# Reordering the head of a two-layer mixer: base chunk 0 ahead of later logits, sums of the weights moved off TensorE, the last group's mixing weights by GpSimd

## The chip, the cores and the metric

One core of one Trainium2 chip. The metric is the device time of one execution, in microseconds; lower is better. The engines are TensorE (PE, with its weight loads as PEld), VectorE (DVE), ScalarE (ACT), GpSimd (POOL) and SyncE (SP), which here only issues DMAs.

## The reference, cut to what matters

Input x has 64 samples of 32 rows (channels) and 512 columns. Two layers are added to it in turn, each a mixing of channels followed by a low-rank expert layer over the columns.

```
# layer 0: mixing weights from the condition of each sample
h = gelu(gelu(cond @ W0 + b0) @ W1 + b1);  att = softmax(h @ W2 + b2)          # [64, 8]
m = einsum('boi,bih->boh', sum_k att[b,k] * weight[k], x) + (att @ bias_k)[:, :, None]
# layer 0: linear layer and top-2 of 8 experts of rank 16
w = softmax over the two largest of  m @ gate_w.T
x = x + m @ base_w.T + base_b + 2 * sum_e w_e * (m @ lora_A[e].T) @ lora_B[e].T
# layer 1: grouped convolution of 9 taps along the columns, plus context, top-2 of 4 experts
m = conv1d(x, weight, groups=4, pad=4) + (cond @ c_weight.T)[:, :, None] + bias
x = x + 4 * sum_e gates_e * (m @ A[e].T) @ B[e].T
```

The mixing acts on the channels and the linear maps on the columns, so they can change places. The kernel multiplies x with `base_w`, `lora_A` and `gate_w` first and mixes the products. The bias of the mixing then contributes the product of a bias per channel and the sum of a weight's rows: the sums over the 512 inputs of `lora_A`/`gate_w` (`lg_sum`), of `base_w` (`sum_w`) and of layer 1's `A`/router (`pj_sum`).

## The kernel before, in words

The 2048 rows (64 samples of 32 channels) are cut into four groups (g or i, 0 to 3) of four tiles (t) of 128 rows; the 512 columns lie in four chunks (c) of 128. x comes in transposed, one DMA for each group and chunk. Nearly all products are taken in a split form: a tile is rounded to a "high" part (on ACT), the rest is the "low" part (VectorE or GpSimd subtract), and `hi_lo` (L959) issues three matmuls, lines L963 to L965. All order is written out by hand: each engine has one queue, waits on counting semaphores, and takes its instructions strictly in the order of the code.

The head, which the change touches, has these steps:

- The attention: `h1`, `h2` and `att` by TensorE with Gelu and Exp on ACT; `keep_busy` (L954) issues products without use between them. `attb` brings the attention weights to 128 partitions.
- `x_logits` (L972): x times lgw in full precision, group 0 only, tile by tile, needing all four chunks of x for each tile. `xl_out` (ACT) evicts them.
- `x_base` (L1020): x times base_w; for group 0 chunk by chunk, from high and low parts (`x_high`, `base_high` on ACT, `x_low`, `base_low` on VectorE). `p0_out` (L442, ACT) evicts it to `p0`.
- `mix_sum` and `mix_half` (L678, L685, VectorE): products of attention and weights and their reduction, which give the mixing matrices of a group; `mix_place` (L502, ACT) puts them into `mixT`. Group 0 is step 1, group 1 step 2, groups 2 and 3 two halves each.
- The sums: lgw by eight matmul instructions with a matrix of ones (L1206), base_w the same way (L1235), copied to a row and turned by L1243, the A/router rows by L1256.
- `mix_logits` (L982) mixes the logits; VectorE adds the bias in `logits` (L690) and runs the gate, `route0` (L698) with one Exp on ACT (`gate_exp`); `turn_lw` (L1034, TensorE line L1037) transposes the result `lw`, `lwT_high` and `lwT_low` split it.
- `x_first` (L998) is the part of the products with x of group 1 that holds the logits.
- `make_y` (L1076): for each chunk four mixes (`mix_base`, L1055) and the experts (`experts0`); `bias_row` (L1058, matmul L1066) makes the bias row. VectorE adds it up in `bias_x` (L717) and `make_x1` (L727). From chunk 2 on, `mix_base` waits for `make_x1` two chunks back.
- `sums` and `sums_low` (L774, L786, VectorE), `x1_high` (ACT) and `x1_low` (L349, GpSimd) prepare `project` (L1083), the first step of layer 1, whose results go through `z_full` (VectorE), `z_high` (ACT) and `z_low` (GpSimd) to `taps` (L1116).
- The weights of layer 1: `az` holds even and odd rows; GpSimd makes the differences `ue` and `ud`, ACT and GpSimd split `sw`, `uw`, `vw`, and the tap and B matrices (`tap_l` L378, `b1_l` L382).
- GpSimd also makes `bias_rows` (L318) and, from group 1 on, `x_low` (L333).

wT lies in the buffer of x1 of group 0, tapw and b1T in that of the output.

## Time and profile before

| | us |
|---|---|
| median of 3 runs | 180.87 (180.74 to 180.99) |
| the profiled execution, its own time | 182.46 |
| its span | 180.7 |
| TensorE busy | 173.0 (96%) |
| VectorE busy | 128.7 (71%) |
| ScalarE busy | 82.0 (45%) |
| GpSimd busy | 83.9 (46%) |

The span runs from the first to the last instruction that the profile shows; the execution's own time holds a little more around it. Busy times are sums of instructions and say nothing of which one others wait for; that is read from the timelines, where each row has a start, a duration, the engine, the line of the code and the tiles, and in brackets the idle time before it with what ended it. A matmul in full precision shows as two instructions, called pieces in the prediction. Mean granted clock of TensorE over the span: 0.991 of full.

### The profile page before, as it was taken

Reading aid. Unit: us, or ns where it says so; the run is one execution under the profiler, and the core shown is the slowest. Engines: PE = TensorE matmul, PEld = TensorE weight load, DVE = VectorE, ACT = ScalarE, POOL = GpSimd, SP = SyncE. Lnnn points to the kernel's source line nnn. Section 1 sums busy time; section 2 is a strip of 40 time slices with the busy share of each in tenths; the row PEclk is TensorE's granted clock in tenths of the full one; section 3 lists DMA queues with packets and bytes.
Section 4 is the critical chain, followed back from the end, with each engine's and each line's share of the span. In section 5 each row is a group of like instructions: output and inputs, shape, how many; then the busy total and the mean of one; then the engine's idle time right before and its main releaser. Section 6 shows DMA issues by size and latency. Waiting matters only on the chain.

```text
span 180.7 us, 3138 instructions
## 1 busy us (share of the span) xinstructions
PE 173.0 (96%) x1125; PEld 161.7 (89%) x1125; DVE 128.7 (71%) x271; ACT 82.0 (45%) x189; POOL 83.9 (46%) x86
## 2 busy tenths in 40 slices
PE   7889999999999999999999999999999999999980
PEld 6778888988998799999989999999899999999870
DVE  1359899968966944797998334987998953368671
ACT  3767656942633546634225176443224464235020
POOL 8023605992065779952007379830006786065000
PEclk9979999999999999999999999999999999999999
DMA  6999100003300240000023000000041000000336
GB/s 174 268 389 387 41 2 0 0 4 123 111 0 4 87 145 2 0 4 0 0 90 147 0 0 4 0 0 0 4 174 58 2 5 0 0 0 0 120 116 232
DMA packets 6495, 12.16 MB, mean 67 GB/s; under 512 B 720, under 2 KB 1360, under 8 KB 6480
## 3 DMA queue, kind: packets, MB, share of 16 engines
q1 hardware_dynamic: 6048, 11.44, 18.1%
q10 hardware_dynamic: 432, 0.52, 0.9%
q8 instruction: 9, 0.15, 0.3%
q14 instruction: 6, 0.05, 0.1%
HBM read 7.77 MB, written 4.19 MB: 66 GB/s over the span
## 4 chain that ended last, share of the span: by engine, by line
PE 86%; DVE 5%; DMA 4%; issue 1%; SPq 1%; DVEq 0%
PE ps L963 21%; PE ps L965 21%; PE ps L964 21%; PE ps L1055 7%; DMA xT_s<-in_xT_dram 4%; PE ps L977 3%; PE ps L994 2%; PE ps L1148 1%; PE ps L1149 1%; PE ps L1037 1%; PE ps L1235 1%; PE ps L1066 1%; DVE xsl L675 1%; DVE xT_s L724 1%; DVE x1T L730 1%
## 5 line engine op out<-in xcount | busy, mean ns | idle before, releaser
L963 PE MATMUL ps<-xw_h,xTh 128*128 128x264 f32 (+1 forms) x96 | 30.4, 317 | 0.0
L964 PE MATMUL ps<-xw_l,xTh 128*128 128x264 f32 (+1 forms) x96 | 29.9, 312 | 0.0
L965 PE MATMUL ps<-xw_h,xTl 128*128 128x264 f32 (+1 forms) x96 | 29.8, 310 | 0.0
L336 POOL TENSOR_TENSOR xTl<-xT_s,xTh 128x512 fp32r<-128x512 f32 x12 | 15.2, 1300 | 24.7 <-ACT xTh L426 16.9
L341 POOL TENSOR_TENSOR zl<-outb,zh 128x340 fp32r<-128x340 f32 x15 | 14.4, 963 | 14.7 <-ACT zh L461 7.8
L352 POOL TENSOR_TENSOR x1Tl<-x1T,x1Th 128x512 fp32r<-128x512 f32 x12 | 16.0, 1346 | 9.4 <-DVE lw L703 9.4
L743 DVE TENSOR_TENSOR outb<-ps,s_sb 128x340 f32<-128x340 f32 x16 | 8.2, 512 | 16.8 <-PE ps L965 12.5
L1055 PEld LDWEIGHTS ps<-mixT,xp 128*128 128x128 f32 x128 | 16.4, 191 | 2.3 <-DVE x1T L730 1.1
L964 PEld LDWEIGHTS ps<-xw_l,xTh 128*128 128x128 f32 x96 | 18.1, 188 | 0.1
L963 PEld LDWEIGHTS ps<-xw_h,xTh 128*128 128x128 f32 x96 | 18.1, 188 | 0.1
L965 PEld LDWEIGHTS ps<-xw_h,xTl 128*128 128x128 f32 x96 | 18.1, 188 | 0.0
L1055 PE MATMUL ps<-mixT,xp 128*128 128x128 f32 x128 | 17.2, 277 | 0.3 <-DVE x1T L730 0.3
L461 ACT ACTIVATE zh<-outb 128x340 fp32r<-128x340 f32 x16 | 7.8, 490 | 17.1 <-DVE outb L743 12.4
L730 DVE SCALAR_TENSOR_TENSOR x1T<-ps,side_s,xT_s 128x512 f32<-128x512 f32 x16 | 12.0, 749 | 4.2 <-PE ps L965 3.6
L352 POOL TENSOR_TENSOR xTl<-x1T,xTh 128x512 fp32r<-128x512 f32 x4 | 6.0, 1502 | 16.9 <-ACT xTh L484 16.9
L724 DVE SCALAR_TENSOR_TENSOR xT_s<-ps,sum_w,xT_s 128x512 f32<-128x512 f32 x16 | 11.7, 744 | 2.8 <-PE ps L1066 2.8
L449 ACT ACTIVATE xp<-ps 128x384 f32<-128x384 f32 x12 | 5.9, 490 | 14.3 <-PE ps L965 14.2
L345 POOL TENSOR_TENSOR zl<-outb,zh 128x272 fp32r<-128x272 f32 x15 | 12.0, 798 | 0.0
L784 DVE TENSOR_TENSOR xs<-x1T 128x256 f32<-128x256 f32 x12 | 10.7, 910 | 0.6
L455 ACT ACTIVATE s_sb<-ps 128x340 f32<-128x340 f32 x16 | 7.1, 442 | 8.6 <-PE ps L965 8.4
L469 ACT ACTIVATE ex<-dif 128x32 f32<-128x32 f32 (+1 forms) x8 | 1.8, 220 | 19.3 <-DVE dif L658 19.3
L324 POOL TENSOR_TENSOR xs<-attT,early_s 8x512 f32<-8x512 f32 x4 | 4.2, 1041 | 11.0 <-ACT attT L527 6.7
(214 smaller groups left out, 507.7 us busy)
## 6 DMA issues: line engine op xcount, KB each, us to landing
xT_s<-in_xT_dram SPq DMA_DIRECT2D x16, 256.0 KB, 4.2
out_dram<-outb SPq DMA_DIRECT2D x14, 256.0 KB, 2.3
x1T<-in_wT_dram SPq DMA_DIRECT2D x4, 256.0 KB, 7.1
x1T<-in_az_dram SPq DMA_DIRECT2D x1, 680.0 KB, 8.4
outb<-in_tapw_dram SPq DMA_DIRECT2D x1, 576.0 KB, 9.2
lgw_s<-in_lgw_dram SPq DMA_DIRECT2D x1, 272.0 KB, 3.4
x1T<-in_lbT_dram SPq DMA_DIRECT2D x1, 256.0 KB, 8.2
outb<-in_b1T_dram SPq DMA_DIRECT2D x1, 256.0 KB, 9.4
```

The costliest lines, as they stand in the source:

```text
L336: nc.gpsimd.tensor_tensor(lo[:, c, :], xT_s[:, g % 2, c, :], hi[:, c, :].bitcast(F32), ALU.subtract).then_inc(x_lo, 1)
L341: nc.gpsimd.tensor_tensor(zl[:, t, 0:QE, :].rearrange("p k e -> p (k e)"), zf[:, t % 2, 0:NE], zh[:, t, 0:QE, :].bitcast(F32).rearrange("p ...
L345: nc.gpsimd.tensor_tensor(zl[:, t, QE:TAPS, :].rearrange("p k e -> p (k e)"), zf[:, t % 2, NE:NE + NO], zh[:, t, QE:TAPS, :].bitcast(F32). ...
L352: nc.gpsimd.tensor_tensor(lo, full, hi.bitcast(F32), ALU.subtract).then_inc(x1_lo, 1)
L724: nc.vector.scalar_tensor_tensor(out=xT_s[:, i % 2, c, :], in0=ps[:, BROW[i], :], scalar=sum_w[:, c:c + 1], in1=xT_s[:, i % 2, c, :], op0= ...
L730: nc.vector.scalar_tensor_tensor(out=x1T[:, i % 2, c, :], in0=ps[:, Y[c], :], scalar=side_s[:, S_BB + c:S_BB + c + 1], in1=xT_s[:, i % 2, ...
L743: nc.vector.tensor_tensor(zf[:, t % 2, 0:NE], ps[:, ring(t, "U"), 0:NE], s_sb[:, t % 2, :], ALU.add).then_inc(ze_ok, 1)
L784: nc.vector.tensor_tensor(full, even, odd, ALU.add).then_inc(xs_ok, 1)
L963: nc.tensor.matmul(dst, sh, mh, start=start and c == 0, stop=False)
L964: nc.tensor.matmul(dst, sh, ml, start=False, stop=False)
L965: last = nc.tensor.matmul(dst, sl, mh, start=False, stop=stop and c == n - 1)
L1055: nc.tensor.matmul(ps[:, Y[c], cols(t)], p0[:, t, cols(c)], mixer(i, t), start=t == 0, stop=False)
```

## The change

- DMA order: each chunk of base_w comes right behind the same chunk of x; then x of group 1, lb, a second, row-wise copy of base_w (`wrow`, four chunks, into the output buffer), az, side. SP then waits for the four sums of wrow (`wsum_ok`) before it issues tapw and b1T, which go into the same buffer.
- TensorE: `keep_busy` is shortened twice from 4 to 2 products and one of 3 is added. `x_logits` goes chunk by chunk: chunk 0, then the two small attention products, then `x_base` chunk 0, and then the later logits. The lgw sum is one matmul (two instructions) of a tile that GpSimd has added up from the four chunks (`lgw_t`), placed behind `x_base` chunk 1. The matmuls L1235 and L1243 are gone. `x_first(1, t)` takes two chunks at a time. The A/router sum is one matmul of `az_t`, also added up by GpSimd; the context matmul moves next to it. `bias_row(1)` moves ahead of `x_base(1, 2)`.
- ACT: order by arrival; the lgw high part goes between the two Gelus; `x_high(1, c)` moves ahead of the gate; `p0_out(0, t)` and `lwT_high(0)` stand ahead of the sums of `wrow` (four Copy activations with an accumulated output); the highs of az come after these; tap and B highs move behind `pj_sum` and four new Identity activations for the context bias, ahead of `x1_high(0, t)`; `sums_high(0, 0..1)` move up between the evictions of group 1.
- GpSimd: the two small sums; `x_low(1, c)` earlier, two of them behind a wait for the first `lw`; the mixing weights of group 3 by a product and three halving additions (from a copy of the attention, `att_last`); `ud` in a buffer of its own; tap and B lows behind `x1_low(0, t)`.
- VectorE: `mix_half(3, ...)`, the context bias, the copy of `sum_w` are gone; a copy to `att_last` is new; x and base lows in pairs by chunk; `bias_x(1, 0)` and `bias_x(1, 1)` move up among the sums.

```diff
@@ SP
             for c in range(DC):
                 load_xT(0, c)
-            sp.dma_start(side_s[:, :], side).then_inc(in_side, 16)
+                sp.dma_start(wT_s[:, c, :], wT[:, c, :]).then_inc(in_base[c], 16)
             for c in range(DC):
-                sp.dma_start(wT_s[:, c, :], wT[:, c, :]).then_inc(in_base[c], 16)
-            sp.dma_start(az_s, az).then_inc(in_az, 16)
+                load_xT(1, c)
             sp.dma_start(lbT_s, lbT).then_inc(in_lb, 16)
             for c in range(DC):
-                load_xT(1, c)
+                sp.dma_start(wrow_s[:, c, :], wrow[:, c, :]).then_inc(in_wrow[c], 16)
+            sp.dma_start(az_s, az).then_inc(in_az, 16)
+            sp.dma_start(side_s[:, :], side).then_inc(in_side, 16)
+            sp.wait_ge(wsum_ok, DC)
@@ GpSimd
             bias_rows(0)
+            pool.wait_ge(base_lo, DC)
+            x_low(1, 0)
+            x_low(1, 1)
+            pool.wait_ge(lw_ok, 1)
+            x_low(1, 2)
+            x_low(1, 3)
+            pool.wait_ge(attl_ok, 1)
+            pool.wait_ge(in_wrep, 16)
+            nc.gpsimd.tensor_tensor(prod_last, att_last[:, :, :].unsqueeze(2).to_broadcast([P, TG, C, K0]),
+                                    wrep_s[:, :, :].unsqueeze(1).to_broadcast([P, TG, C, K0]), ALU.mult).then_inc(tree_ok, 1)
+            pool.wait_ge(tree_ok, 1)
+            nc.gpsimd.tensor_tensor(prod_last[:, :, :, 0:4], prod_last[:, :, :, 0:4], prod_last[:, :, :, 4:8],
+                                    ALU.add).then_inc(tree_ok, 1)
...
+            nc.gpsimd.tensor_tensor(agg[:, TG * (G - 1):TT, :], prod_last[:, :, :, 0], prod_last[:, :, :, 1],
+                                    ALU.add).then_inc(aggl_ok, 1)
...
+            pool.wait_ge(lw_ok, 2)
+            for t in range(TG):
+                x1_low(0, t)
             pool.wait_ge(tap_hi, 1)
...
-            pool.wait_ge(lw_ok, 2)
-            for t in range(TG):
-                x1_low(0, t)
@@ ACT
+            for c in range(DC):
+                act.wait_ge(in_wrow[c], 16)
+                nc.scalar.activation(wrow_s[:, c, :], wrow_s[:, c, :], ACT.Copy,
+                                     accum_out=sum_w[:, c:c + 1]).then_inc(wsum_ok, 1)
...
             nc.scalar.activation(pj_sum[:, :], psum_b, ACT.Copy).then_inc(pjsum_ok, 1)
+            act.wait_ge(in_side, 16)
+            for j in range(BT):
+                rows = slice(j * C, (j + 1) * C)
+                last = nc.scalar.activation(ctxbias[rows, :], ctx_b[rows, j:NB:BT], ACT.Identity,
+                                            bias=side_s[rows, S_FS:S_FS + 1])
+            last.then_inc(ctx_ok, 1)
+            act.wait_ge(in_tap, 16)
+            nc.scalar.activation(tap_h[:, :, :].rearrange("p k c -> p (k c)"), tapw_s, ACT.Copy).then_inc(tap_hi, 1)
+            act.wait_ge(in_b1, 16)
+            nc.scalar.activation(b1_h[:, :], b1T_s, ACT.Copy).then_inc(b1_hi, 1)
             for t in range(TG):
                 x1_high(0, t)
@@ VectorE
             sums(0, 0)
             sums(0, 1)
+            bias_x(1, 0)
             lwT_low(1)
-            bias_x(1, 0)
             sums_low(0, 0)
             sums(0, 2)
+            bias_x(1, 1)
             sums_low(0, 1)
             sums(0, 3)
             make_x1(1, 0)
             sums_low(0, 2)
             sums_low(0, 3)
-            for c in range(1, DC):
-                bias_x(1, c)
-                make_x1(1, c)
+            make_x1(1, 1)
+            bias_x(1, 2)
+            make_x1(1, 2)
+            bias_x(1, 3)
+            make_x1(1, 3)
@@ TensorE
-            for c in range(DC):
-                last = nc.tensor.matmul(ps[:, LGS, 0:LG], ones[:, :], lgw_s[:, c, :], start=c == 0, stop=c == DC - 1)
-            last.then_inc(lgsum_mm, 1)
             keep_busy(4, 2)
-            x_logits(0, (0,))
+            x_logits(0)
...
-            x_logits(0, (1,))
-            x_logits(1)
+            keep_busy(4, 3)
+            for t in range(TG):
+                x_base(0, t, (0,))
...
+            for c in range(1, DC):
+                x_logits(c)
             for t in range(TG):
                 x_base(0, t, (1,))
+            pe.wait_ge(xl_ok, 2)
+            pe.wait_ge(lgt_ok, 1)
+            nc.tensor.matmul(ps[:, LGS, 0:LG], ones[:, :], lgw_t[:, 2, :], start=True, stop=True).then_inc(lgsum_mm, 1)
...
-            pe.wait_ge(base_lo, DC)
-            for n, part in enumerate((base_h, base_l)):
-                for c in range(DC):
-                    last = nc.tensor.matmul(ps[:, BSUM, :], ones_r[:, :], part[:, c, :],
-                                            start=n + c == 0, stop=n == 1 and c == DC - 1)
-            last.then_inc(bsum_mm, 1)
```

## Rows read from the trace of the kernel before

**Rows 1.** The page: shares of the span in the chain that ended last.
```profile
PE 86%; DVE 5%; DMA 4%; issue 1%; SPq 1%; DVEq 0%
```

**Rows 2.** Waits of TensorE, 0 to 50 us: total, times, longest.
```profile
PE ps L977 <- DMA xT_s<-in_xT_dram: 1.3, 2, 1.1
```

**Rows 3.** TensorE in half microseconds: busy, PEclk (granted clock), DMA share, GB/s.
```profile
11.00:11.50 0.50, 0.50 (x2) 0.50 0.97 382
```

**Rows 4.** Timeline of TensorE, 0 to 32 us: start, duration, line, tiles, count.
```profile
9.38 0.50 PE L977 MATMUL ps<-lgw_s,xT_s 128*128 128x136 f32 x2 [1.10 <-DMA xT_s<-in_xT_dram]
...
10.93 4.69 PE L977 MATMUL ps<-lgw_s,xT_s 128*128 128x136 f32 x24
...
16.15 0.47 PE L963 MATMUL ps<-xw_h,x1Th 128*128 128x512 f32 x1
...
21.79 1.09 PE L994 MATMUL ps<-xp,mixT 128*128 128x136 f32 x8
...
31.18 0.66 PE L1037 MATMUL ps<-ident,lw 128*128 128x128 f32 x4
```

**Rows 5.** Timeline of VectorE, 0 to 66 us.
```profile
8.02 1.28 DVE L675 TENSOR_TENSOR x1Tl<-xT_s,x1Th 128x512 fp32r<-128x512 f32 x2
...
19.77 1.98 DVE L675 TENSOR_TENSOR xw_l<-lgw_s,xw_h 128x544 fp32r<-128x544 f32 x1
22.45 1.15 DVE L695 SCALAR_TENSOR_TENSOR xp<-lg_sum,mixbias,ps 128x136 f32<-128x136 f32 x4 [0.71 <-PE ps L994]
...
26.77 0.69 DVE L703 TENSOR_TENSOR lw<-xp,w 128x512 f32<-128x512 f32 x1
...
49.58 0.19 DVE L665 SCALAR_TENSOR_TENSOR kept<-rank,ex 128x32 f32<-128x32 f32 x1
...
50.47 0.69 DVE L703 TENSOR_TENSOR lw<-xp,w 128x512 f32<-128x512 f32 x1
51.08 1.85 DVE L784 TENSOR_TENSOR xs<-x1T 128x256 f32<-128x256 f32 x2
```

**Rows 6.** Timeline of TensorE, 31 to 66 us.
```profile
37.55 1.05 PE L1055 MATMUL ps<-mixT,xp 128*128 128x128 f32 x8
...
46.51 0.42 PE L963 MATMUL ps<-xw_h,xTh 128*128 128x384 f32 x1
...
52.94 0.60 PE L1037 MATMUL ps<-ident,lw 128*128 128x128 f32 x4
...
63.19 0.31 PE L963 MATMUL ps<-sw_h,xsh 128*128 128x340 f32 x1
```

**Rows 7.** The chain that ended last, in order of time: start, share of time.
```profile
22.88 1.85 PE ps L1235 x8
...
30.28 0.98 PE ps L1243 x8
...
45.81 0.89 PE ps L1256 x8
```

**Rows 8.** Timeline of ACT, 0 to 16 us.
```profile
5.74 1.28 ACT L522 ACT_TABLE_LOAD   x1
...
7.29 1.14 ACT L426 ACTIVATE x1Th<-xT_s 128x512 fp32r<-128x512 f32 x2
```

**Rows 9.** Timeline of GpSimd, 14 to 66 us.
```profile
19.51 1.65 POOL L356 TENSOR_TENSOR sw_l<-x1T,sw_h 128x680 fp32r<-128x680 f32 x1
28.98 5.04 POOL L336 TENSOR_TENSOR xTl<-xT_s,xTh 128x512 fp32r<-128x512 f32 x4 [7.82 <-DVE lb_l L675]
...
36.92 1.04 POOL L324 TENSOR_TENSOR xs<-attT,early_s 8x512 f32<-8x512 f32 x1
37.93 2.63 POOL L378 TENSOR_TENSOR tap_l<-outb,tap_h 128x1152 fp32r<-128x1152 f32 x1
...
51.24 5.32 POOL L352 TENSOR_TENSOR x1Tl<-x1T,x1Th 128x512 fp32r<-128x512 f32 x4 [9.44 <-DVE lw L703]
```

**Rows 10.** Timeline of GpSimd, 64 to 105 us.
```profile
66.45 0.92 POOL L341 TENSOR_TENSOR zl<-outb,zh 128x340 fp32r<-128x340 f32 x1 [1.04 <-ACT zh L461]
```

More of the change, by code:

```diff
@@ L42, with two_layer_mixer @@
 S_CTX, S_FS, S_BB, S_N = 0, 128, 129, 133
-def two_layer_mixer(nc: bass.Bass, xT, early, wrep, lgw, wT, lbT, az, tapw, b1T, side, out):
+def two_layer_mixer(nc: bass.Bass, xT, early, wrep, lgw, wT, wrow, lbT, az, tapw, b1T, side, out):
     with ExitStack() as ctx:
@@ L215, in two_layer_mixer @@
         in_base = [sem(f"in_base{c}") for c in range(DC)]
+        in_wrow = [sem(f"in_wrow{c}") for c in range(DC)]
         xT_in = [[sem(f"xT_in{a}{c}") for c in range(DC)] for a in range(2)]
@@ L517, in _ @@
                                  bias=early_s[:, A_B0:A_B0 + 1]).then_inc(h1_ok, 1)
+            act.wait_ge(in_lgw, 16)
+            nc.scalar.activation(xw_h[:, :, 0:LG], lgw_s[:, :, :], ACT.Copy).then_inc(lgw_hi, 1)
             act.wait_ge(h2_mm, 1)
@@ L577, in _ @@
             p0_out(1, 3)
-            for t in range(TG):
-                sums_high(0, t)
+            sums_high(0, 2)
+            sums_high(0, 3)
             for i in range(1, G - 1):
@@ L816, in _ @@
                                            op0=ALU.mult, op1=ALU.mult).then_inc(att_ok, 1)
-            for c in range(DC):
-                x_low(c)
+            x_low(0)
             base_low(0)
+            x_low(1)
+            base_low(1)
             dve.wait_ge(attb_mm, 1)
@@ L831, in _ @@
             last.then_inc(mixb_ok, 1)
-            dve.wait_ge(in_side, 16)
-            for j in range(BT):
-                rows = slice(j * C, (j + 1) * C)
-                last = nc.vector.tensor_scalar(ctxbias[rows, :], ctx_b[rows, j:NB:BT],
-                                               side_s[rows, S_FS:S_FS + 1], None, ALU.add)
-            last.then_inc(ctx_ok, 1)
-            dve.wait_ge(lgw_hi, 1)
-            minus(xw_l[:, :, 0:LG], lgw_s[:, :, :], xw_h[:, :, 0:LG]).then_inc(lgw_lo, 1)
+            x_low(3)
+            base_low(3)
             for t in range(TG):
@@ L969, in mixer, with x_logits @@
                 return mixT[:, TG * i + t, :, :].rearrange("p j o -> p (j o)")
-            def x_logits(half, tiles=(0, 1)):
+            def x_logits(c):
                 pe.wait_ge(in_lgw, 16)
-                for t in (2 * half + a for a in tiles):
-                    for c in range(DC):
-                        pe.wait_ge(xT_in[0][c], 16)
-                        last = nc.tensor.matmul(ps[:, XLG[half], lg_cols(t)], xT_s[:, 0, c, cols(t)], lgw_s[:, c, :],
-                                                start=c == 0, stop=c == DC - 1)
-                if tiles[-1]:
-                    last.then_inc(xl_mm, 1)
+                pe.wait_ge(xT_in[0][c], 16)
+                for t in range(TG):
+                    last = nc.tensor.matmul(ps[:, XLG[t // 2], lg_cols(t)], xT_s[:, 0, c, cols(t)], lgw_s[:, c, :],
+                                            start=c + t % 2 == 0, stop=c == DC - 1 and t % 2 == 1)
+                    if c == DC - 1 and t % 2:
+                        last.then_inc(xl_mm, 1)
             def mix_logits(i, t):
@@ L1240, in _ @@
                     x_base(0, t, (c,))
-            pe.wait_ge(bsum_ok, 1)
-            for c in range(DC):
-                last = nc.tensor.matmul(ps[:, WSUM, c:c + 1], row_w[0:1, cols(c)], ones[0:1, 0:1], start=True, stop=True)
-            last.then_inc(wsum_mm, 1)
             turn_lw(0)
-            for c in range(DC):
+            for chunks in ((0, 1), (2, 3)):
                 for t in range(TG):
-                    x_first(1, t, (c,))
+                    x_first(1, t, chunks)
             make_y(0)
@@ L1251, in _ @@
                 mix_logits(1, t)
-            pe.wait_ge(in_az, 16)
+            pe.wait_ge(azt_ok, 1)
+            pe.wait_ge(in_side, 16)
             pe.wait_ge(x1_ok, DC)
-            for m in range(2):
-                for h in range(2):
-                    last = nc.tensor.matmul(psum_b, ones[:, :], az_s[:, m, h, 2 * PJ:3 * PJ],
-                                            start=m + h == 0, stop=m + h == 2)
-            last.then_inc(pjsum_mm, 1)
+            nc.tensor.matmul(ctx_b, side_s[:, S_CTX:S_CTX + P], early_s[:, A_COND:A_COND + NB],
+                             start=True, stop=True).then_inc(ctx_mm, 1)
+            nc.tensor.matmul(psum_b, ones[:, :], az_t[:, 2, :], start=True, stop=True).then_inc(pjsum_mm, 1)
             x_base(1, 0)
             x_base(1, 1)
+            bias_row(1)
             x_base(1, 2)
@@ L1263, in _ @@
             x_base(1, 3)
-            bias_row(1)
             for i in range(1, G - 1):
@@ L1367 @@
     nc = _bacc.Bacc("TRN2", target_bir_lowering=False, num_devices=1)
-    for name, v in (("xT", xT), ("early", early), ("wrep", wrep), ("lgw", lgw), ("wT", wT), ("lbT", lbT),
+    for name, v in (("xT", xT), ("early", early), ("wrep", wrep), ("lgw", lgw), ("wT", wT), ("wrow", wrow), ("lbT", lbT),
                     ("az", az.reshape(P, 2, 2, NE)), ("tapw", tapw.reshape(P, TAPS * P)), ("b1T", b1T), ("side", side)):
```

144 lines of the change are left out of this document (74 added, 70 removed).

## The prediction, made before the changed kernel ran

> **What bounds the kernel now.** I read the chain that ended last first, then the waits of TensorE, its granted clock in half microseconds, and the timelines of the four engines over the first 66 us. 86% of the chain is on TensorE [rows 1]. So what leaves TensorE's queue in the head is gained, as long as nobody else becomes late. Its longest wait after the constants is 1.3 us on two transfers of x [rows 2]. From 11.0 to 14.0, six half microseconds on end, the granted clock is 0.50, the 1.2 GHz level; before it fell TensorE had stood for 1.10 us, to 9.38 [rows 3, 4]. 24 pieces of the x logits take 4.69 us there; at full clock 8 pieces of the same width (L994) take 1.09 with the last one's tail, 0.12 each, so 24 would take 2.8 [rows 4]. The head therefore holds three kinds of gain: work for sums (L1206, L1235, L1243, L1256), waits, and a stretch at half clock.
>
> Beyond the head stand three chains that TensorE only just doesn't see. They decide here. (1) First gate: VectorE starts logits(0) at 22.45 and ends lw(0) at 26.77 + 0.69 = 27.46, while TensorE turns it at 31.18 [rows 4, 5]: 3.7 us of slack. (2) Second gate: lw(1) ends at 50.47 + 0.69 = 51.16 and is turned at 52.94 [rows 5, 6]: 1.8 us of slack. (3) From 51.16 to the projection of group 0, which starts at 63.19 [rows 6], are 12.0 us, in which VectorE makes the x1 of group 1 and GpSimd its lows.
>
> **TensorE's own work.** Removed: the eight L1235 pieces, 1.85 us of the chain, and the eight L1243, 0.98 us [rows 7]. The sum of the A/router rows goes from eight pieces in 0.89 us [rows 7] to two, 0.22; the sum over lgw from eight pieces that lay ahead of the wait for x, so were hidden, to two at 0.12 each on the path, 0.25. The context matmul is moved, not removed: even. Sum: 1.85 + 0.98 + 0.67 - 0.25 = 3.3 us. The removed row copy and sum_w copy go from ACT and VectorE; in their place ACT sums four 128x512 tiles.
>
> **The head walked anew.** Transfers: x chunk 0 keeps its place, base chunk 0 takes that of x chunk 1, which was in before 7.8 (ACT has copied two chunks from 7.29 in 1.14 us [rows 8]); x chunk 1 takes the place of chunk 2, 9.38 by the wait. After that a chunk of 0.262 MB comes each 0.69, at the 382 GB/s of rows 3: five more of x and base by 12.8, then four of x of group 1, lb and four of wrow by 19, az and side by 21. x_logits(0) runs from about 6.4; the attention vectors are unchanged (bounded by the table load at 5.74, 1.28 us [rows 8]), so the two small products of att run at 7.9 to 8.6. VectorE makes x_low(0) at 8.02 and then base_low(0), 0.64 each, to 9.3 [rows 5]. x_base chunk 0 can thus start at 9.35 instead of 16.15. I take the clock as full: the two idle stretches are 0.5 us each, with three keep_busy products between, against one of 1.1 us before. From 9.35: twelve pieces of 512 columns, 2.8 (two chunks take 5.6, 16.15 to 21.79 [rows 4]); mixb 0.36; 24 pieces of logits 2.8; chunk 1 2.8; the lgw sum 0.25; so mix_logits(0) at 18.35 and logits(0) on VectorE at 19.0 (0.66 behind, as 22.45 behind 21.79 [rows 4, 5]). VectorE's queue ahead of them (from 8.0 eight lows, 5.1, and the mix sum with two small copies, at the estimate of its 1024 elements twice 3.4) ends near 17, in time. lw ends 5.0 later, at 24.0 (before 27.46: **+3.4 us**). TensorE wants it at 24.95 (chunks 2 and 3 are 5.6 more). p0's evictions follow each tile at about 0.7 and hold nobody; x_first with two chunks at a time needs only x_low(1,0..1), made by GpSimd before.
>
> Then TensorE: 6.4 to make_y(0) (31.18 to 37.55), from there 9.0 to x_base(1,0) at 46.51 [rows 4, 6], less 0.67 for the shorter sum and with 0.25 for the context: 24.95 + 6.4 + 8.5 = 39.9. On TensorE alone that is 6.6 us gained. The wrow sums on ACT (four of 512 elements at 0.57 with an accumulator read, some 0.7 each, from 26.3 to 29.1) are ready before bias_x(0,0) at 33. SP now waits for them; behind that wait stand tapw and b1T and every later transfer of x and out. tapw and b1T have 13 us until ACT asks for them at 42, the next x isn't due before x1 at 34: cost nothing; if ACT's sums came 10 us later they would hold tap_h.
>
> **GpSimd's chain, the new bound.** Its cost: 2.63 us for 1152 elements and 5.04 / 4 = 1.26 for 512 [rows 9] give 2.14 ns an element and 0.16 fixed. After lw(0) at 24.0 it does, in order: x_low(1,2..3) 2.5; the last group's products and three halving adds, 1024 + 512 + 256 + 128 elements, 4.8, and 0.3 for their three waits on each other; ue, ud, az_t twice, sw_l, uw_l, vw_l, 3332 elements in seven instructions, 8.2; bias_rows(1) 1.04. It ends at 24.0 + 16.9 = 40.9. (Before, it was done with this at 37.96 [rows 9], far ahead of the second gate.) ACT waits for it with bias_high(1), and behind that stand, in its queue: pj_sum, the four context biases that were VectorE's, tap_h, b1_h, x1_high of four tiles and only then gate_exp(1). I take 0.55 + 0.15 + 4 x 0.2 + 1.07 + 0.53 + 2.1 (four tiles at 0.53, as the two x_high [rows 8]) + 0.25 = 5.5: exp at 46.4. VectorE's rest of the gate is 49.58 to 51.16 = 1.6 [rows 5]: lw(1) at 48.0. From lw(0) that is 24.0 against 23.7 before: **-0.3 us**. TensorE wants turn_lw(1) at 39.9 + 6.4 (46.51 to 52.94 [rows 6]) + 0.4 for the moved bias_row = 46.7, so it stands 1.3 us here: a wait in the place of the removed work.
>
> The short products with inner rows of four and two elements are not in the trace. Bounds: the rate above (4.8) as lower end, and one and a half to twice it for the three adds (up to 2.4 more); the nearest row is the plain rate and I take it. An Identity activation isn't there either: below by 0.2 each as the small activations, above by two table loads of 1.28 [rows 8], 2.6 in all; the nearest rows are the copies behind Exp, which have none (the x_high at 7.29), so I take none. The Trainium skill, "ScalarE: Activation LUTs" (Table sets: the hidden batching unit), says that cheap functions such as copy and identity are in every set; by that rule it is none as well, and for Identity no run here shows it yet.
>
> **VectorE held by GpSimd.** Before, VectorE's lgw low took 1.98 us for 544 elements, where 512 take 0.64: it was issued at 19.77, and GpSimd's sw_l ran to 19.51 + 1.65 = 21.16 [rows 5, 9]. The two sums of 256 at 51.08 took 1.85, as GpSimd began x1_low at 51.24. So, by these rows, a VectorE instruction with both inputs in SBUF waits for the end of the GpSimd instruction in flight. The Trainium skill, "GPSIMD Engine Reference" (Key points), says that the two engines contend where VectorE has two SBUF inputs; the trace agrees (1.98 against 0.7 us), and this rule speaks against the change.
>
> Moved behind x1_low(0) are tap_l (2.63) and b1_l (1.28), which ran from 37.93 on, when VectorE read PSUM. Before, GpSimd was free at 56.56 (51.24 + 5.32 [rows 9]), and nothing of its own lay beside VectorE's sums_low after that until x_low(2). Now, with W = lw(1): sums 0 and 1 to W+1.85; bias_x(1,0); lwT_low to W+3.85; sums_low 0 at W+4.2 to 4.55; sums 2 behind x1_low's end, to W+6.0; bias_x(1,1) to 6.7; sums_low 1 behind tap_l, to 8.8; sums 3 behind b1_l, to 10.3; make_x1(1,0) to W+11.0. TensorE turns lw at W (0.5), has x_base(1,3) done at W+2.65 (6.4 / 3 each), and after two of the four mixes, at 1.6 each, needs that x1 at W+5.85. It waits 5.1 us. Then mixes 2 and 3 cost 1.6 each, and the projection starts at W+14.25 = 62.25, where it was W+12.0 before: **-2.25 us**.
>
> Sum: 3.4 - 0.3 - 2.25 = +0.9 us, the projection at 62.3 instead of 63.19. From there both kernels have the same work. The profiled execution of before took 182.46 us by its own time (span 180.7); the sum makes that 181.6. The median 180.87 lies 1.6 below it; the forecast for the median is 180.87 - 0.9 = **180.0 us**.
>
> **Rivals.** (a) VectorE is held less (it gets in between GpSimd's instructions, or tap_l has been overtaken): the projection starts near W+10 = 58. Then GpSimd is the bound: x1_low 5.3, tap_l and b1_l 3.9, x_low(2) 5.1, context 0.64, so its first z_low comes at W+14.9 = 62.9 instead of 66.45 [rows 10], and the taps need its last. Gain 3.5: 177.4. For it: only two clear cases of holding are in the rows. Against: both took the whole length of the other's instruction. (b) Slower: GpSimd's chain between the gates costs more than 24.0, by short rows in the halving adds and by mutual holding with bias_low, lb_l and the gate. Place: ACT standing at bias_high(1), TensorE at turn_lw(1). It decides from 0.9 us more on; with 2.4 more, lw(1) is at 50.4 and the time 182.4. For it: 5 us of new work on an engine that is busy without a break for 17 us. Against: its rows are steady, four x_low in 5.04 us and four x1_low in 5.32 [rows 9]. (c) The clock falls in the head in spite of keep_busy: another 3.3 us at half rate delay everything by 1.65, 181.65. For it: TensorE still has nothing in two places before 9.35, and before one such gap came ahead of the fall.
>
> **How the numbers follow.** Forecast 0.45 (own range 179.0 to 181.1), (a) 0.25, (b) 0.20, (c) 0.10. The range takes in most of (a) and the lighter half of (b): 177.3 to 181.9. A measurement here tells 0.2%, 0.36 us, from nothing. Faster: 0.32 of the forecast's 0.45, all of (a), 0.01 of (c): 0.58. Slower: 0.05, 0.19 of (b), 0.06 of (c): 0.30. Within: 0.12.
>
> **What would show it.** turn_lw(0) at 25 instead of 31.2 with clock 1.00 all through (the head); GpSimd without a break from 24 to 41, with the four tree steps near 5.1 us; TensorE idle 1 to 2 us before the second turn_lw and some 5 us before the third mix of group 1, its releaser make_x1 on VectorE; sums_low and sums of 0.42 us drawn out to 1.2 and more, one past 2 us beside tap_l. The forecast is wrong if TensorE goes through make_y(1) without a wait (then a), if the second turn_lw comes later than 49 (then b), or if the first comes later than 26 (then c or late transfers).

## The result: slower by 2.2%, and the profile after

| | before | after |
|---|---|---|
| median, us | 180.93 (180.20 to 181.65, 6 runs) | 186.66 (184.89 to 188.19, 6 runs) |
| profiled execution, us: its span | 180.7 | 183.6 |
| mean granted clock over the span | 0.991 | 0.977 |
| TensorE busy, us | 173.0 | 170.6 |
| GpSimd busy, us | 83.9 | 92.2 |

The ratio of after to before is 1.0218, 95% interval 1.0178 to 1.0259. It is made of the lower of the two lots in which the times of after lie, 184.9 to 185.4 and 187.9 to 188.2; the medians of all six executions differ by 3.2%. The profiled execution took 185.38. Forecast were 180.0 us and a range that ended at 181.9.

The chain that ended last, in shares of the span, for [rows 1]:

```profile
PE 62%; POOL 11%; DVE 8%; ACT 6%; issue 6%; DMA 4%; SPq 1%; DVEq 0%; POOLq 0%; ACTq 0%
```

TensorE had 86% of the chain before and has 62% now: a quarter of the chain went to engines that stood beside it before. Which waits these are is in the view of TensorE's waits (total, times, longest), for [rows 2]:

```profile
PE ps L1100 <- DVE x1T L778: 4.3, 1, 4.3
PE ps L1081 <- DVE lw L751: 1.3, 1, 1.3
...
PE ps L1038 <- ACT xp L473: 0.5, 1, 0.5
```

The wait for x is gone in this execution (in those of e1_tap_early and e2_fill, whose head is the same, it is back with 0.6 and 1.0 us). Two long waits stand in its place, at the second gate (for lw) and at the third mix of group 1 (for make_x1(1,0)). TensorE's timeline, for [rows 4, 6] (start, duration, tiles; in brackets the idle time before):

```profile
12.88 3.05 PE L1021 MATMUL ps<-lgw_s,xT_s 128*128 128x136 f32 x24
...
25.24 0.60 PE L1081 MATMUL ps<-ident,lw 128*128 128x128 f32 x4
...
49.46 0.66 PE L1081 MATMUL ps<-ident,lw 128*128 128x128 f32 x4 [1.31 <-DVE lw L751]
...
54.06 1.05 PE L1100 MATMUL ps<-mixT,xp 128*128 128x128 f32 x8
...
60.14 2.08 PE L1100 MATMUL ps<-mixT,xp 128*128 128x128 f32 x8 [4.33 <-DVE x1T L778]
...
63.29 1.91 PE L1100 MATMUL ps<-mixT,xp 128*128 128x128 f32 x8
...
66.11 0.32 PE L1008 MATMUL ps<-sw_h,xsh 128*128 128x340 f32 x1
```

The first turn of lw comes at 25.24 instead of 31.18, the projection of group 0 at 66.11 instead of 63.19. The 2.9 us between the two projections are the whole difference of the spans; behind them both kernels run alike. The mixes took 1.05 us ahead of the long wait and 2.08 and 1.91 behind it. The windows of half a microsecond say why (TensorE busy, granted clock, DMA share, GB/s), for [rows 3]:

```profile
58.50:59.00 0.50, 0.00 (x0) 1.00 0.00 0
59.00:59.50 0.50, 0.00 (x0) 0.56 0.00 0
...
60.50:61.00 0.50, 0.50 (x4) 0.50 0.00 0
...
65.50:66.00 0.50, 0.50 (x3) 0.61 0.50 180
66.00:66.50 0.50, 0.50 (x5) 1.00 0.50 184
```

The clock fell to its 1.2 GHz level inside the wait, at 59.1, and stayed there to 65.9. VectorE and GpSimd over the same stretch, for [rows 5, 9]:

```profile
48.72 0.69 DVE L751 TENSOR_TENSOR lw<-xp,w 128x512 f32<-128x512 f32 x1
49.33 1.84 DVE L832 TENSOR_TENSOR xs<-x1T 128x256 f32<-128x256 f32 x2
...
53.94 1.31 DVE L832 TENSOR_TENSOR xs<-x1T 128x256 f32<-128x256 f32 x1
...
55.84 2.18 DVE L723 TENSOR_TENSOR xsl<-xs,xsh 128x256 fp32r<-128x256 f32 x1
58.12 1.30 DVE L832 TENSOR_TENSOR xs<-x1T 128x256 f32<-128x256 f32 x1
59.34 0.74 DVE L778 SCALAR_TENSOR_TENSOR x1T<-ps,side_s,xT_s 128x512 f32<-128x512 f32 x1
```

```profile
27.52 2.41 POOL L386 TENSOR_TENSOR x1T<-att_last,wrep_s 128x1024 f32<-128x1024 f32 x1
30.02 1.61 POOL L389 TENSOR_TENSOR x1T<-x1T 128x512 f32<-128x512 f32 x1
...
41.00 1.04 POOL L334 TENSOR_TENSOR xs<-attT,early_s 8x512 f32<-8x512 f32 x1
49.49 5.48 POOL L362 TENSOR_TENSOR x1Tl<-x1T,x1Th 128x512 fp32r<-128x512 f32 x4 [7.44 <-DVE lw L751]
54.93 2.81 POOL L415 TENSOR_TENSOR tap_l<-outb,tap_h 128x1152 fp32r<-128x1152 f32 x1
57.70 1.44 POOL L419 TENSOR_TENSOR b_l<-outb,b_h 128x512 fp32r<-128x512 f32 x1
```

Sums of 256 elements, 0.42 us by themselves, took 1.31 beside the last x1_low, 2.18 beside tap_l and 1.30 beside b1_l (the row b_l), and make_x1(1,0), on which TensorE's third mix waits, stands behind all of them.

### The profile page after: what moved, and what is told of

Same layout as the page of the kernel before. It is cut to its first block, busy times and chain, and to the rows that moved or that the text cites. A ratio compares the mean times of both kernels' runs of the same rounds, so it can differ in the third digit from the quotient of the medians.

```text
span 183.6 us, 3096 instructions
## 1 busy us (share of the span) xinstructions
PE 170.6 (93%) x1096; PEld 158.9 (87%) x1096; DVE 129.4 (70%) x263; ACT 85.6 (47%) x200; POOL 92.2 (50%) x94
## 4 chain that ended last, share of the span: by engine, by line
PE 62%; POOL 11%; DVE 8%; ACT 6%; issue 6%; DMA 4%; SPq 1%; DVEq 0%; POOLq 0%; ACTq 0%
PE ps L1008 16%; PE ps L1009 16%; PE ps L1010 16%; PE ps L1100 6%; DMA x1T<-in_wT_dram 4%; POOL xTl L346 3%; DVE xsl L723 2%; POOL x1T L386 1%; PE ps L1194 1%; PE ps L1195 1%; ACT x1Th L517 1%; DVE xs L832 1%; PE ps L1038 1%; POOL sw_l L366 1%; POOL x1T L389 1%
## 5 line engine op out<-in xcount | busy, mean ns | idle before, releaser
L346 POOL TENSOR_TENSOR xTl<-xT_s,xTh 128x512 fp32r<-128x512 f32 x12 | 15.7, 1338 | 26.8 <-ACT xTh L459 23.0
L1100 PEld LDWEIGHTS ps<-mixT,xp 128*128 128x128 f32 x128 | 18.3, 208 | 6.5 <-DVE x1T L778 5.1
L1100 PE MATMUL ps<-mixT,xp 128*128 128x128 f32 x128 | 19.1, 296 | 4.4 <-DVE x1T L778 4.3
L832 DVE TENSOR_TENSOR xs<-x1T 128x256 f32<-128x256 f32 x12 | 12.4, 1056 | 0.6
L488 ACT ACTIVATE s_sb<-ps 128x340 f32<-128x340 f32 x16 | 7.1, 442 | 10.7 <-PE ps L1010 10.6
L522 ACT ACTIVATE xsh<-xs 128x256 fp32r<-128x256 f32 x12 | 5.0, 419 | 13.5 <-DVE xs L832 13.4
```

The source lines that it names most:

```text
L346: nc.gpsimd.tensor_tensor(lo[:, c, :], xT_s[:, g % 2, c, :], hi[:, c, :].bitcast(F32), ALU.subtract).then_inc(x_lo, 1)
L832: nc.vector.tensor_tensor(full, even, odd, ALU.add).then_inc(xs_ok, 1)
L1100: nc.tensor.matmul(ps[:, Y[c], cols(t)], p0[:, t, cols(c)], mixer(i, t), start=t == 0, stop=False)
```

## The experiments

All but e14_before_again were timed beside the kernel before on the same chip, whose median there was 180.5 to 180.7. Ratios are to it, with their 95% intervals; the changed kernel's is 1.0218 (1.0178 to 1.0259). The intervals of e1, e2, e3, e5b, e6 and e10 overlap with that, so what these runs show is read from their traces and not from their times. The first three ask what the two waits and the clock cost.

**e1_tap_early: tap_l and b1_l ahead of GpSimd's wait for lw(1)**

```
 bias_rows(1)
-pool.wait_ge(lw_ok, 2); x1_low(0, 0..3)
 tap_l; b1_l
+pool.wait_ge(lw_ok, 2); x1_low(0, 0..3)
```

> The changed kernel with tap_l and b1_l back ahead of GpSimd's wait for the second lw, where GpSimd stands idle from 42.0 to 49.5. Theory (VectorE's two-SBUF-input instructions are held by GpSimd's instruction in flight): tap_l now begins at 45.0, when ACT has tap_h, and holds one step of the gate, so the second lw comes at about 50.4 instead of 49.4; behind it only x1_low holds, sums_low 1 takes under 1 us instead of 2.18, and make_x1(1,0) comes 7.5 us after lw instead of 9.9. TensorE's wait ahead of the third mix falls from 4.3 to about 2.3 us and the projection starts near 62 instead of 66.1: about 4 us faster than the changed kernel, about 181.3. Rival (VectorE's own queue is simply too long and GpSimd has no part in it): the wait stays over 4 us and the time stays at 185.

Measured: 184.28 us, ratio 1.0210 (1.0139 to 1.0282). The long wait is gone (0.55 us left), but it came up elsewhere: tap_l now runs from 45.30 to 48.0, beside the second gate. VectorE's timeline:

```profile
45.38 2.90 DVE L705 TENSOR_TENSOR above<-xp 128x256 f32<-128x256 f32 x1
48.31 1.13 DVE L706 TENSOR_TENSOR dif<-xp,top 128x32 f32<-128x32 f32 x1
```

An instruction of 0.42 us, issued as GpSimd's began, ended 0.3 us behind its end. lw(1) ends at 52.11, TensorE waits 3.8 us for it and runs part of x_base(1,3) and a mix at half clock behind the wait. So the same two GpSimd instructions cost either the gate or the sums, by where they stand. The 181.3 us that I expected are missed by 3 us: I had lw(1) 1.0 us later, and it came 2.7 later, and I had no half clock behind TensorE's wait for it.

**e2_fill: 36 products of ones ahead of the third mix, in the wait**

```
+if i == 1 and c == 2:
+    keep_busy(4, 36)
```

> The changed kernel with 36 products without use on TensorE ahead of the third mix of group 1, about as long as its wait of 4.3 us there. Theory (the fall of the granted clock behind this wait costs 2.8 us on top of it): no half clock between 59 and 66, make_x1(1,0) unmoved at 59.3 to 60.1, the four mixes in 0.9 instead of 1.9 us, the projection at 63.3 instead of 66.1 and 182.3 us. Rival (the clock isn't what lengthens the stretch, VectorE and ACT are): projection at 66, time at 185.

Measured: 183.81 us, ratio 1.0175 (1.0097 to 1.0252). TensorE's timeline:

```profile
57.42 4.47 PE L1001 MATMUL ps<-ones_r 128*128 128x256 f32 x36
62.01 1.16 PE L1102 MATMUL ps<-mixT,xp 128*128 128x128 f32 x8
```

The mix behind is at full clock again. From the first turn of lw to the projection are 38.3 us, 40.9 in the changed kernel: 2.6 of the 2.8 expected. This execution's turn_lw(0) came 1.7 us later than the changed kernel's, at 26.98, which hides a part of the gain in its time. Why is in the rows of its head, which has the code of the changed kernel's (TensorE's timeline, then its windows of a microsecond):

```profile
7.91 1.34 PE L1021 MATMUL ps<-lgw_s,xT_s 128*128 128x136 f32 x8 [0.98 <-DMA xT_s<-in_xT_dram]
```

```profile
9.00:10.00 1.00, 1.00 (x6) 0.50 1.02 283
...
11.00:12.00 1.00, 1.00 (x4) 0.50 1.01 297
```

Here the clock fell in the head, behind a wait of 0.98 us for x. That is the prediction's rival (c), which did not come in the profiled execution of the changed kernel.

**e3_dve_order: VectorE's make_x1(1,0) and (1,1) ahead of the sums of rows 2 and 3**

```
 sums_low(0, 0)
-sums(0, 2)
 bias_x(1, 1)
-sums_low(0, 1); sums(0, 3)
 make_x1(1, 0)
-sums_low(0, 2); sums_low(0, 3)
 make_x1(1, 1)
+sums(0, 2); bias_x(1, 2); sums_low(0, 1); sums(0, 3); make_x1(1, 2)
+bias_x(1, 3); sums_low(0, 2); make_x1(1, 3); sums_low(0, 3)
```

> The changed kernel with make_x1(1,0) and (1,1) moved ahead of sums 2 and 3 on VectorE; nothing is taken from GpSimd. Theory (it is the place of make_x1 behind four held instructions that makes TensorE wait): make_x1(1,0) ends near 55, TensorE doesn't wait in make_y(1), the clock stays full, the projection starts near 59.2. Then GpSimd is late: x_low of group 2 waits for ACT, which waits for sums 3, so its first z_low comes near 66.4 instead of 69.4, and the taps of group 0 start 3 us earlier than in the changed kernel, with a wait ahead of them: 182. Rival (GpSimd isn't late behind it): 178.5.

Measured: 185.51 us, ratio 1.0258 (1.0210 to 1.0306). No wait is left in the mixes, and the projection comes at 61.13. Nothing of it reaches the end: 182 was expected. A part of the miss is this execution's head, which was 2.3 us late (turn_lw(0) at 27.55). The rest is in TensorE's waits:

```profile
PE ps L1008 <- POOL zl L351: 3.6, 1, 3.6
```

This is the prediction's rival (a): as soon as VectorE isn't late, GpSimd is, which does tap_l, b1_l and x_low(2) between x1_low and the first z_low, and stands 1.9 us ahead of x_low(2) for ScalarE. The taps wait 3.6 us for the last z_low.

**e6_tap_split: tap_l as nine instructions of 128 elements, at its place**

```
-nc.gpsimd.tensor_tensor(tap_l[all 1152], ...)
+for k in range(TAPS): nc.gpsimd.tensor_tensor(tap_l[:, k, :], ...)
```

> The changed kernel with GpSimd's subtraction of tap_l written as nine instructions of 128 elements in place of one of 1152. In the trace of the changed kernel VectorE's two-input sums_low(0,1) took 2.18 us beside that 2.81 us instruction and its sums_low(0,0) 0.71, where 0.41 is its time alone. Theory H (VectorE's instruction with two inputs in SBUF waits for the end of the one GpSimd instruction in flight): sums_low(0,1) falls from 2.18 to about 0.8 us, make_x1(1,0) comes 1.3 us earlier than the 10.7 us behind the end of lw(1), TensorE's wait ahead of the third mixed row falls from 4.3 to about 3.0 us, and nine fixed costs of some 0.16 us add 1.3 us to GpSimd; the time is 0 to 1.5 us below the changed kernel's 186. Theory S (the two engines share the way to SBUF by turns, whatever the length of an instruction): sums_low(0,1) keeps 2.0 to 2.3 us, the wait stays at 4.3 us and the time at 185 to 187.

Measured: 183.63 us, ratio 1.0151 (1.0104 to 1.0198). VectorE's sums_low(0,1) and GpSimd's instructions beside it:

```profile
58.00 0.44 DVE L724 TENSOR_TENSOR xsl<-xs,xsh 128x256 fp32r<-128x256 f32 x1
```

```profile
57.09 4.70 POOL L416 TENSOR_TENSOR tap_l<-outb,tap_h 128x128 fp32r<-128x128 f32 x9
```

This is the cleanest reading of all: the same data, the same engines, the same work side by side, and 2.18 us became 0.44 when the neighbour's instruction became short. Theory H holds, S falls. The Trainium skill, "SBUF — State Buffer" (Summary: rules for kernel authors), says the same: where VectorE has two SBUF inputs while the GpSimd instruction reads SBUF, the second one to issue blocks fully until the first finishes. By that rule the length of the one instruction decides, and the trace agrees (2.18 and 0.44 us). TensorE's third mix:

```profile
59.75 1.16 PE L1101 MATMUL ps<-mixT,xp 128*128 128x128 f32 x8 [1.77 <-DVE x1T L779]
61.44 1.07 PE L1101 MATMUL ps<-mixT,xp 128*128 128x128 f32 x8
```

The wait fell to 1.77, below the 3.0 expected, and behind it the clock is whole. From the end of lw(1), 51.57, to the projection at 63.05 are 11.5 us, where the changed kernel had 16.7. Of these 5.2 us, 3.0 came back behind the projection, 2.2 of them as waits at the taps (1.7, for z_low) and at turn_mw (0.5), and this execution's head was 2.1 late.

**e5b_tree_late: GpSimd's product tree behind bias_rows(1)**

```
 x_low(1, 2); x_low(1, 3)
-tree of the last group (4 instructions)
 ue ... vw_l; bias_rows(1)
+tree of the last group (4 instructions)
 act: mix_place(3) behind p0_out(1, 1), was ahead of xa_out(1, 0)
 dve: its wait for the tree ahead of make_x1(1, 0), was ahead of make_x1(0, 2)
```

The product lies in a later buffer of x1T; with a buffer of its own the kernel doesn't fit into SBUF and gives no time.

> The changed kernel with the last group's product tree on GpSimd moved behind bias_rows(1), its product kept in a later buffer of x1T, and mix_place(3) moved behind p0_out(1,1) on ScalarE. In the trace of the changed kernel the tree took 2.41 + 1.61 + 0.61 + 0.41 = 5.0 us on GpSimd ahead of ue, and bias_rows(1) ended at 42.04. Theory G (the tree's place in GpSimd's queue made lw(1) late): bias_rows(1) ends near 37.2, the wait of 0.5 us at mix_logits(1) is gone, ScalarE's own work ahead of exp (p0_out, x1_high) is now last, lw(1) ends near 48.0 in place of 49.4, and the time is 1.0 to 1.8 us below the changed kernel's, where the tree then delays x1_low only if it is not done at lw(1)'s end. Theory R (rival: lw(1) is set by ScalarE's queue alone): lw(1) stays at 49.2 to 49.6 and the time within 0.5 us of the changed kernel's. The wait ahead of the third mixed row stays at 4 us or more in both.

Measured: 184.32 us, ratio 1.0192 (1.0155 to 1.0229). bias_rows(1) ends at 37.96, the 0.5 us wait is gone, lw(1) ends at 47.75, and the third mix comes 1.66 us earlier, though this execution's head was 0.66 late. The third mix still waits 4.32 us and takes 2.08. Theory G holds for the second gate. The 0.5 us wait, at the mix logits, isn't shown to be the tree's alone: the same edit takes mix_place(3) out of ScalarE's way to xa_out(1).

**e13_tree_tap: both repairs**

Edit: those of e5b_tree_late and e6_tap_split.

> The changed kernel with the two repairs that its traces point to and nothing else of its order touched: the product tree behind bias_rows(1) with mix_place(3) behind p0_out(1,1), and tap_l as nine instructions of 128 elements. Alone the first made TensorE's turn_lw(1) 1.65 us earlier (47.81 for 49.46), the second cut the wait ahead of the third mixed row from 4.33 to 1.77 us and left no half-clock stretch behind it (from the end of lw(1) to projection 11.5 us in place of 16.7), of which 1.7 + 0.5 us came back as waits at the taps and at turn_mw. Theory (the two causes are separate and add): third mix wait 1.5 to 2 us at the full clock, projection near 59.5 if the head runs at the full clock, some 2 us given back at the taps: span 178.5 to 180, time 180.3 to 182, 4.5 us below the changed kernel. Rival (they don't add: the wait that one removes is filled by the next): 182.5 to 184.5, like either alone.

Measured: 181.59 us, ratio 1.0030 (0.9999 to 1.0062). TensorE's waits:

```profile
PE ps L1011 <- POOL zl L351: 2.4, 1, 2.4
PE ps L1103 <- DVE x1T L782: 1.8, 1, 1.8
```

The projection is at 59.55, at full clock. The two causes are separate and add. From the first turn of lw to the projection the changed kernel takes 40.87 us; e5b is 2.46 below that, e6 5.20, and both together 7.55. In the time they take back nearly all that the change lost (1.0030). TensorE now stands 2.4 us at the taps, for z_low.

**e11_no_tree: the last group's weights on VectorE again, nothing else undone**

```
-tree on GpSimd
+mix_half(3, 0); mix_half(3, 1)   # VectorE, behind make_x1(0, 3)
 act: mix_place(3) stays ahead of xa_out(1, 0)
```

> The changed kernel with one part undone: the last group's mixing weights are mixed on VectorE behind make_x1(0,3) again, and GpSimd has no product tree; the head's order and VectorE's sums stay as the change has them. In the changed kernel's trace the tree held VectorE's lb_l for 2.91 us in place of 0.69 and made bias_rows(1) end at 42.04. Theory G (what the tree costs is its place on GpSimd): bias_rows(1) ends near 37, but VectorE has two mix_half more, 2.8 us, ahead of bias_low(1), so lw(1) ends near 48.2 in place of 49.4; the sums beside x1_low and tap_l still take 2 us, the wait ahead of the third mixed row stays at 4 us with the half clock behind it: 184 to 185.5, like the version with the tree moved back (184.3). Rival R (the tree on GpSimd gains as much on VectorE as it costs): 185.5 to 187.5.

Measured: 189.31 us, ratio 1.0422 (1.0345 to 1.0499): a miss by 4 us. ScalarE's timeline, and TensorE's:

```profile
34.45 1.31 ACT L526 ACTIVATE mixT<-late 32x128 f32<-32x128 f32 x4 [0.97 <-DVE late L715]
43.60 1.30 ACT L526 ACTIVATE mixT<-late 32x128 f32<-32x128 f32 x4 [7.84 <-DVE late L715]
44.92 1.24 ACT L460 ACTIVATE xp<-ps 128x264 f32<-128x264 f32 x4
```

```profile
45.37 2.18 PE L1020 MATMUL ps<-xp,mixT 128*128 128x136 f32 x8 [5.36 <-ACT xp L460]
```

I had walked VectorE's and GpSimd's queues and not ScalarE's. In the changed order mix_place(3) stands ahead of xa_out(1), without which mix_logits(1) can't start; with VectorE's late product ScalarE stood 7.8 us. So this run says nothing of GpSimd's tree against VectorE's. It does say that a moved producer needs its consumer moved on every queue, and it shows a second long wait of TensorE (5.36 us) with half clock behind it (0.50 from 45 to 51.5).

**e10_head_fill: seven more products ahead of x_logits(0)**

```
-keep_busy(4, 2)
+keep_busy(4, 9)
```

> The changed kernel with keep_busy(4, 2) ahead of x_logits(0) made keep_busy(4, 9): seven more products of 128 rows of ident, 0.8 us of work at the full clock, in the head. In two of three profiles of versions of the changed kernel the head's rows from 9 to 12 us took twice as long (keep_busy x3 1.01 us, L1021 x8 2.02) and everything behind came 1.7 to 2.3 us later; the changed kernel's times also lie in two lots, 185 and 188. Theory C (TensorE's waits in the reordered head sometimes cost it its full clock, and more work there holds it): the times fall into one lot near 185 to 186, the spread within 1 us, median 0 to 1.5 us below the changed kernel's 186.7. Rival N (the head's clock has another cause, or more work in the waits does not hold it): two lots as before, 185 and 188, and with work that is not hidden the median 0 to 0.8 us above it.

Measured: 186.03 us (184.90 to 187.29), ratio 1.0298 (1.0240 to 1.0357). The spread of 2.4 us stays, so more products ahead of x_logits(0) did not make the times even: rival N, though its two lots can't be seen in four times. The cause of the head's two speeds stays open. The trace shows one thing more. TensorE's wait at the third mix is the changed kernel's (4.31 us), but the low clock lasts 3.4 us there, from 60.4 to 63.8, and not 6.8: the third mix takes 2.07 us, the fourth 1.10, and from the end of the wait to the projection are 4.8 us, where the changed kernel had 6.0.

**e14_before_again: the kernel before, a second profile**

> The kernel before once more, unchanged, for a second profile. In the first profile TensorE ran its 24 logits products from 10.93 to 15.62 at the half clock (4.69 us; 3.05 at the full clock in the changed kernel), and the span was 180.7; most executions of this kernel beside the experiments had spans of 178.4 to 179.7. Theory (the first profile was of an execution whose head ran at the half clock, which others don't): this one, if its span is under 179.5, shows x24 at about 3.1 us, turn_lw(0) near 29.5 in place of 31.18 and projection near 61.3 in place of 63.19. Rival (the head of this kernel always has the half clock, and the spread is elsewhere): x24 at 4.7 us whatever the span.

Measured: 180.50 us, span 178.8. TensorE's timeline, beside [rows 4, 6]:

```profile
10.19 3.05 PE L977 MATMUL ps<-lgw_s,xT_s 128*128 128x136 f32 x24
...
29.25 0.66 PE L1037 MATMUL ps<-ident,lw 128*128 128x128 f32 x4
...
61.25 0.31 PE L963 MATMUL ps<-sw_h,xsh 128*128 128x340 f32 x1
```

The 24 pieces that took 4.69 us in the first profile take 3.05, and turn_lw(0) and the projection come 1.93 and 1.94 us earlier. The whole difference between the two executions of the same kernel lies in the head: the 24 pieces start 0.74 us earlier, as the wait for x is 0.2 us and not 1.1, they take 1.64 less at the full clock, and 0.45 is lost again before the turn. lw(1) ends at 48.54 + 0.69 = 49.23, and the projection is 12.0 behind it, as in the first.

**e9_best, e12_best_z and e15_best_order: a version that uses what was found**

```
 head and VectorE's early order as in the change; make_x1 as in e3_dve_order
-tree on GpSimd
+mix_half(3, .) on VectorE behind make_x1(0, 3); mix_place(3) behind p0_out(1, 1)
+tap_h, b1_h ahead of mix_place(2); tap_l, b1_l right behind bias_rows(1)
+gate_exp(1) ahead of x1_high; x_high(2, .) ahead of sums_high(0, 2)
 e12: z_low(0, 0..3), then x1_low(1, 0..3)
 e15: x1_low(1, 0), z_low 0, 1, x1_low 1, z_low 2, 3, x1_low 2, 3; x1_high(1, 0) first
```

> A version that keeps the part of the change that worked (base_w chunk 0 ahead of the later logits, sums over the part rows on VectorE early, so that turn_lw(0) starts near 25 us in place of 31) and takes back or moves the rest: the last group's mixing weights are mixed on VectorE behind make_x1(0,3) as in the kernel before (GpSimd has no tree), tap_l and b1_l are made right behind bias_rows(1) while GpSimd would wait for lw(1), their high parts on ScalarE ahead of mix_place(2); gate_exp(1) stands ahead of x1_high, x_high(2,c) ahead of the last two sums_high of group 0, mix_place(3) behind p0_out(1,1), and make_x1(1,0) and (1,1) ahead of the sums of rows 2 and 3. Theory (each of the losses of the changed kernel has the cause named): lw(1) ends near 48.4, no wait over 1 us ahead of the third mixed row and no half-clock stretch there, projection near 58 in place of 63.2 in the kernel before, time 174 to 177. Rival (a): VectorE then runs ahead of GpSimd's z_low and x_low(2), TensorE waits 2 to 4 us at the taps, time 178 to 180. Rival (c): the head falls to the half clock in some executions, 2 us more in these.

Measured: 180.14 us, ratio 0.9955 (0.9913 to 0.9998). lw(1) ends at 47.95 and the projection is at 57.67, as expected. The time isn't: TensorE waits 1.56 us at the taps for the last z_low, behind x1_low(1,.) on GpSimd, and against the second profile of before (61.25) the lead was 3.6 us and not the 5.5 that it is against the first.

> The combined version (180.1 us; its trace: lw(1) ends 47.95, no wait ahead of the third mixed row, projection at 57.67, full clock, but 1.6 us of TensorE's wait at 73.03 for z_low on GpSimd, which does x1_low(1,t), 1.3 us each, between the z_low of rows t) with the four z_low of group 0 ahead of the four x1_low(1,t) on GpSimd. Theory: z_low of row 3 then ends near 69.5 and the wait at 73 is gone; the span falls by 1.5 us, the time to 178 to 179.2. Rival (a'): x1_low(1,t), now later, hold something behind them (bias_rows(2) and logits of group 2 near 82) and the wait only moves: 179.5 to 180.5.

Measured: 179.82 us, ratio 0.9956 (0.9924 to 0.9988). The wait only moved, as the rival had it. VectorE's timeline beside four x1_low in a row, which GpSimd did from 72.48 to 78.24:

```profile
72.72 1.51 DVE L715 TENSOR_TENSOR xsl<-xs,xsh 128x256 fp32r<-128x256 f32 x1
74.33 1.32 DVE L824 TENSOR_TENSOR xs<-x1T 128x256 f32<-128x256 f32 x1
75.58 2.94 DVE L715 TENSOR_TENSOR xsl<-xs,xsh 128x256 fp32r<-128x256 f32 x2
```

Each is held to the end of one x1_low; route1 and with it turn_mw are 1.7 us late.

> The combined version with GpSimd's order in the second group as x1_low(1,0), z_low 0, z_low 1, x1_low(1,1), z_low 2, z_low 3, x1_low(1,2), x1_low(1,3), and x1_high(1,0) ahead of z_high(0,0) on ScalarE. In the first combined version (180.1 us) TensorE waited 1.6 us at the taps for z_low of row 3, in the second (179.8) 1.7 us at turn_mw, because four x1_low in a row held VectorE's sums_low(1,2..3) for 1.5 and 2.9 us. Theory: z_low of row 3 ends near 72 and only two x1_low, 2.9 us, stand beside VectorE's sums, so that both waits are under 0.6 us: span 176 to 177, time 178 to 178.8. Rival: with x1_low(1,0) released only by make_x1(1,3) at 61.5, z_low of row 0 starts 0.6 us later and all z_low behind it, and VectorE's sums are held as before: 179.3 to 180.2.

Measured: 178.28 us (177.46 to 180.13), ratio 0.9863 (0.9827 to 0.9898). TensorE's waits and the order on GpSimd:

```profile
PE ps L1078 <- DVE lw L750: 0.7, 1, 0.7
PE ps L1212 <- DVE mwT L722: 0.5, 1, 0.5
PE ps L1097 <- ACT xp L479: 0.3, 1, 0.3
```

```profile
69.51 1.12 POOL L351 TENSOR_TENSOR zl<-outb,zh 128x340 fp32r<-128x340 f32 x1
70.59 0.95 POOL L355 TENSOR_TENSOR zl<-outb,zh 128x272 fp32r<-128x272 f32 x1
71.50 2.91 POOL L362 TENSOR_TENSOR x1Tl<-x1T,x1Th 128x512 fp32r<-128x512 f32 x2
```

The wait at the taps is gone, that at turn_mw is 0.2 us, the span is 175.7. This version is 1.4% faster than the kernel before and beats the changed one by more than 3%. So the head can stay as the change has it, and what the change lost is won back in the order of the other queues. How much of the 1.4% is the head's isn't shown: against the second profile of before, lw(1) ends 1.3 us earlier (47.91 for 49.23) and the projection comes 3.65 earlier (57.60 for 61.25), so 2.3 us are gained between the two, where VectorE's new order works, and no run puts that order on the kernel before.

## Why the prediction was wrong, step by step

1. **The head walked anew: right.** Forecast for lw(0) was 24.0, it ended at 24.44; turn_lw(0) 24.95 against 25.24.
2. **GpSimd's chain: right in kind, mis-sized.** The tree took 5.25 us from 27.52 to ue at 32.77, forecast 5.1. Of it the first halving add cost 1.61 for 512 outputs in rows of four, where the plain rate gives 1.26. bias_rows(1) ended at 42.04 for 40.9: 0.44 from the later lw(0), 0.55 from x_low(1,2..3), 0.15 from the tree. ScalarE's 5.5 us to exp were 5.43, the four Identity without a table load (1.08 us in all). lw(1) ended at 49.41 for 48.0: **1.4 us**. Of these, 1.1 came down from bias_rows(1); the other 0.3 are Exp itself (47.51 to 47.83), which my sum left out.
3. **VectorE held by GpSimd: right to 0.2 us.** make_x1(1,0) ended at 60.08 = W+10.7 for W+11.0. The third mix came at W+10.7 for W+10.95.
4. **"Then mixes 2 and 3 cost 1.6 each": this step failed.** From the end of the wait to the projection they took 5.97 us together and not 3.3, since the clock fell inside the wait. I had foreseen the wait of 5.1 us and priced it as time only. I had even read in [rows 3, 4] that the clock was at half behind a stand of 1.10 us, and kept the fall as a rival for the head alone, with 1.1 us of idle, and not for a wait four times as long. **2.7 us**, shown by e2_fill (the same wait filled: 2.6 us back) and e6_tap_split (the wait shortened: mixes at 1.16 and 1.07). The size is that of this execution: behind the same wait e10_head_fill lost 1.5 us.
5. **The sum made against the profiled execution and then taken off the median: failed as well.** That execution was 1.6 us above the median. The second profile, e14_before_again, of an execution of 180.50 us, has a projection 1.94 us earlier, and all of that lies in the head, in the stretch that the change rewrites at full clock. So an execution near the median did not have them to lose. Against the second profile my own numbers give 62.25 - 61.25: 1.0 us slower, 181.5, and against the first 181.6. The sign of the forecast came from this step. **1.6 us.**

The terms, from 180.0: 1.4 + (2.7 - 0.2) + 1.6 = 5.5 gives 185.5, and the profiled execution took 185.4. The median of all six times is 1.3 above that; what makes the difference was not caught in a profile of this kernel. Profiles of versions with this head show one candidate, a head of which x_logits(0) takes 2.0 us and not 1.1 and that ends 0.7 to 2.3 us later (e3, e5b, e6, e11, e12 and e13), with turn_lw(0) at 25.9 to 27.6.

Rival (b) had the second gate's price (lw(1) 1.4 late of up to 2.4), rival (a) was shown by e3_dve_order as what comes next. Rival (c) named the mechanism, a clock that falls behind a wait, for the head alone. There it is seen in e2_fill (turn_lw(0) 1.7 us late, where I had priced 1.65); in the profiled execution it came at the third mix instead.
